# Row maxima of attention scores from 64 contraction rows, two heads as a pair of matmuls on the two halves of the rows

## What is computed

```python
k = jnp.concatenate([k_c, k_rb], axis=-1)      # 32 content + 32 position numbers per head
q = jnp.concatenate([q_c, q_rb], axis=-1)
scores = jnp.einsum('bhsd,bhtd->bhst', q, k) / math.sqrt(HEAD_DIM)
attn = jax.nn.softmax(scores, axis=-1)
ctx = jnp.einsum('bhst,bhtd->bhsd', attn, v_c)
```

## Time and profile before

| | |
|---|---|
| median of 3 runs | 1858.47 us (1858.25 to 1858.62) |
| the profiled execution | 1858.86 us |
| its span in the trace | 1857.0 us, so 1.9 us lie around it |
| mean granted TensorE clock | 0.946 of full speed |
| PE, DVE, ACT, POOL busy over the span | 92%, 56%, 45%, 39% |
| attention | from the start to about 1081 us |

### The profile page before, as it was taken

One profiled execution on the slowest core, in us unless ns is written; L12 is line 12 of the kernel. 1 busy time (PEld: TensorE's weight loads), 2 busy tenths in 40 slices (PEclk: granted clock), 3 DMA queues, 4 the chain that ended last, 5 costly groups with the idle time before them and its releaser, 6 DMA issues.

```text
span 1857.0 us, 21713 instructions
## 1 busy us (share of the span) xinstructions
PE 1703.8 (92%) x7194; PEld 1042.3 (56%) x7194; DVE 1030.8 (56%) x2133; ACT 828.4 (45%) x1465; POOL 726.6 (39%) x627
## 2 busy tenths in 40 slices
PE   5898989989989989989899788999999999988998
PEld 2444535435445445444444346888766666656886
DVE  2666577567676685684755635444511111116998
ACT  2345355355355454454454434443133333336554
POOL 0355465456455455563655642000122222214341
PEclk9798999989989999999989889999799999999999
DMA  5654455356355364462554332412473333448773
GB/s 157 174 155 123 121 143 181 84 152 181 86 165 152 93 187 123 136 190 77 150 162 150 100 114 79 164 46 97 132 264 131 126 127 132 127 141 299 240 240 123
DMA packets 123365, 270.51 MB, mean 146 GB/s; under 512 B 14996, under 2 KB 26644, under 8 KB 117108
## 3 DMA queue, kind: packets, MB, share of 16 engines
q1 hardware_dynamic: 96856, 205.93, 36.7%
q0 software_dynamic: 12912, 41.82, 7.1%
q10 hardware_dynamic: 13488, 21.37, 3.1%
HBM read 153.99 MB, written 92.01 MB: 132 GB/s over the span
## 4 chain that ended last, share of the span: by engine, by line
PE 66%; DVE 22%; DMA 4%; ACT 3%; issue 3%; POOL 1%; SPq 1%; DVEq 0%; ACTq 0%; POOLq 0%
PE bank L616 9%; PE bank L594 8%; PE bank L672 7%; PE bank L695 7%; DVE a L804 6%; PE bank L553 6%; PE bank L536 5%; PE bank L476 5%; DVE a L810 3%; PE bank L521 3%; PE bank L507 3%; PE bank L525 3%; PE bank L492 2%; PE bank L545 2%; DVE a L735 2%
## 5 line engine op out<-in xcount | busy, mean ns | idle before, releaser
L1449 POOL TENSOR_TENSOR a<-a 128x512 f32<-128x512 f32 x384 | 483.0, 1284 | 475.2 <-ACT a L1261 475.2
L1261 ACT ACTIVATE a<-bank 128x512 f32<-128x512 f32 x512 | 299.8, 595 | 258.2 <-PE bank L525 252.0
L804 DVE TENSOR_REDUCE a<-bank 128x1 f32<-128x512 f32 x512 | 325.2, 668 | 96.4 <-PE bank L507 95.9
L521 PE MATMUL bank<-a 128*128 128x512 f32 x512 | 281.6, 550 | 50.1 <-ACT a L1261 50.0
L507 PE MATMUL bank<-a 128*128 128x512 f32 x512 | 203.0, 434 | 28.5 <-DVE a L804 20.1
L525 PE MATMUL bank<-a 68*128 68x512 f32 x512 | 209.4, 409 | 0.3 <-ACT a L1251 0.2
L594 PE MATMUL bank<-c 128*128 128x512 f32 x768 | 186.8, 401 | 22.8 <-ACT c L1306 8.4
L521 PEld LDWEIGHTS bank<-a 128*128 128x128 f32 x512 | 100.1, 196 | 180.1 <-ACT a L1261 98.8
L1116 DVE TENSOR_TENSOR f<-f 128x256 f32<-128x256 f32 x79 | 33.6, 425 | 268.2 <-ACT f L1378 268.2
L594 PEld LDWEIGHTS bank<-c 128*128 128x128 f32 x768 | 146.2, 192 | 62.3 <-issue 13.2
L616 PE MATMUL bank<-c 128*128 128x512 f32 x768 | 176.8, 390 | 3.4 <-DVE c L854 1.7
(11 more groups left out here) (176 smaller groups left out, 2093.7 us busy)
## 6 DMA issues: line engine op xcount, KB each, us to landing
a<-kq_scratch SPq DMA_DIRECT2D x192, 256.0 KB, 5.6
kq_scratch<-a SPq DMA_DIRECT2D x32, 1024.0 KB, 4.1
a<-a SPq DMA_DIRECT2D x80, 256.0 KB, 5.0
yp_scratch<-f ACTq DMA_DIRECT2D x79, 256.0 KB, 2.0
a<-in_L_attn_x SPq DMA_DIRECT2D x15, 1024.0 KB, 8.5
x_scratch<-a SPq DMA_DIRECT2D x8, 1024.0 KB, 5.1
h_scratch<-a SPq DMA_DIRECT2D x8, 1024.0 KB, 4.3
hT_scratch<-a SPq DMA_DIRECT2D x8, 1024.0 KB, 6.5
```

The source lines that it names most:

```text
L521: e.matmul(SC[n % 2][:], K.Kc[:, z, j, i * P:(i + 1) * P], K.Qc[:, z, j, :], start=True, stop=False)
L804: e.tensor_reduce(K.mx[:, i, j:j + 1], K.MX[n % 3][:], AX.X, ALU.max).then_inc(Z.max, 1)
L1261: e.activation(K.pt[:, n % NP, :], K.SC[n % 2][:], ACT.Exp, scale=SCALE).then_inc(Z.exp, 1)
L1449: e.tensor_tensor(K.acc[:, j, :], a, K.pt[:, n % NP, :], ALU.add).then_inc(Z.acc, 1)
```

## The change

The first pass takes only high parts: 32 content rows and 32 position rows, 64 in all. The stacks are laid out by the parity of the head, so that an even head has these 64 rows in partitions 0 to 63 and an odd head has them in 64 to 127; the other half holds the two remaining products. A `top` now covers two heads: two matmuls of 64 rows, the first on the lower half and the second on the upper half of the rows, into two of the three banks. It waits once for the reduction that frees the second of the two banks, and DVE makes two reductions behind it. There are 8 pairs per unit in place of 16 tops. `scores` reads the same stacks as before, whose rows are only in another order. `send` issues 14 transfers in place of 8, with the same bytes.

```diff
+STACK = 14
 # attention_order, before the first unit and inside a unit
-    out += [("top", 0, j, i) for j in range(4) for i in range(4)] + [("rows", 0)] + norm_order("n", 1)
+    out += [("top", 0, j, i) for j in (0, 2) for i in range(4)] + [("rows", 0)] + norm_order("n", 1)
...
-        tops = [(j, i) for j in range(4) for i in range(4)] if u + 1 < NU else []
+        tops = [(j, i) for j in (0, 2) for i in range(4)] if u + 1 < NU else []
...
-            while nt < len(tops) and nt < (step + 1) * 5 // 4 + 2:
+            while nt < len(tops) and nt < (step + 1) * 5 // 8 + 1:
...
 # PE
     def top(u, j, i):
-        z, n = u % RS, 16 * u + 4 * j + i
-        if n >= 3:
-            w.wait_ge(Z.max, n - 2)
-        w.wait_ge(Z.stack[z], 8 * 16 * (u // RS + 1))
-        e.matmul(MX[n % 3][:], K.Qc[:, z, j, i * P:(i + 1) * P], K.Kc[:, z, j, :], start=True, stop=True).then_inc(Z.top, 1)
+        z, n = u % RS, 16 * u + 4 * j + 2 * i
+        if n:
+            w.wait_ge(Z.max, n - 1)
+        w.wait_ge(Z.stack[z], STACK * 16 * (u // RS + 1))
+        for c in range(2):
+            half = slice(64 * c, 64 * c + 64)
+            e.matmul(MX[(n + c) % 3][:], K.Qc[half, z, j + c, i * P:(i + 1) * P], K.Kc[half, z, j + c, :],
+                     start=True, stop=True).then_inc(Z.top, 1)
...
 # DVE
     def top(u, j, i):
-        n = 16 * u + 4 * j + i
-        w.wait_ge(Z.top, n + 1)
         if u:
             m = K.fill["rows", u - 1]
             w.wait_ge(Z.full[m % 2], m // 2 + 1)
-        e.tensor_reduce(K.mx[:, i, j:j + 1], K.MX[n % 3][:], AX.X, ALU.max).then_inc(Z.max, 1)
+        for c in range(2):
+            n = 16 * u + 4 * j + 2 * i + c
+            w.wait_ge(Z.top, n + 1)
+            e.tensor_reduce(K.mx[:, i, j + c:j + c + 1], K.MX[n % 3][:], AX.X, ALU.max).then_inc(Z.max, 1)
...
 # SP, send(u)
-        rep = lambda r: raw(K.krx[r:r + HD, y, :].unsqueeze(1).broadcast_to([HD, 4, S]))
+        rep = lambda r: raw(K.krx[r:r + HD, y, :].unsqueeze(1).broadcast_to([HD, 2, S]))
...
-        e.dma_start(raw(K.Kc[96:128, z, :, :]), rep(0)).then_inc(Z.stack[z], 16)
-        e.dma_start(raw(K.Qc[96:128, z, :, :]), rep(32)).then_inc(Z.stack[z], 16)
-        piece = lambda n: K.kq_d[z, :, n, :].rearrange("(j p) s -> p j s", j=4)
+        for t, r in ((K.Kc, 0), (K.Qc, 32)):
+            e.dma_start(raw(t[32:64, z, 0::2, :]), rep(r)).then_inc(Z.stack[z], 16)
+            e.dma_start(raw(t[64:96, z, 1::2, :]), rep(r)).then_inc(Z.stack[z], 16)
+        piece = lambda n, heads: K.kq_d[z, :, n, :].rearrange("(j p) s -> p j s", j=4)[:, heads, :]
         w.wait_ge(Z.kq[z], 16 * (u // RS + 1))
-        for t, k, n in ((K.Kc, 0, 0), (K.Kc, 1, 0), (K.Kc, 2, 1), (K.Qc, 0, 2), (K.Qc, 1, 3), (K.Qc, 2, 2)):
-            e.dma_start(raw(t[HD * k:HD * k + HD, z, :, :]), piece(n)).then_inc(Z.stack[z], 16)
+        even, odd, every = slice(0, 4, 2), slice(1, 4, 2), slice(0, 4)
+        for t, k, n, heads in ((K.Qc, 0, 2, every), (K.Kc, 0, 0, even), (K.Kc, 3, 0, odd), (K.Qc, 3, 2, every), (K.Kc, 0, 1, odd),
+                               (K.Kc, 1, 0, odd), (K.Qc, 1, 3, odd), (K.Kc, 2, 0, even), (K.Qc, 2, 3, even), (K.Kc, 3, 1, even)):
+            e.dma_start(raw(t[HD * k:HD * k + HD, z, heads, :]), piece(n, heads)).then_inc(Z.stack[z], 16)
```

More of the change, by code:

```diff
@@ L779, in proj @@
             u = NG * (b - 2) + 3
-            w.wait_ge(Z.stack[u % RS], 8 * 16 * (u // RS + 1))
+            w.wait_ge(Z.stack[u % RS], STACK * 16 * (u // RS + 1))
             w.wait_ge(Z.KR[z], 4 * 16 * (b // 2))
@@ L1572, in send @@
         if u >= RS:
-            w.wait_ge(Z.stack[z], 8 * 16 * (u // RS))
+            w.wait_ge(Z.stack[z], STACK * 16 * (u // RS))
         e.dma_start(K.kq_d[z], raw(K.kq[:])).then_inc(Z.kq[z], 16)
-        rep = lambda r: raw(K.krx[r:r + HD, y, :].unsqueeze(1).broadcast_to([HD, 4, S]))
+        rep = lambda r: raw(K.krx[r:r + HD, y, :].unsqueeze(1).broadcast_to([HD, 2, S]))
         w.wait_ge(Z.rope, 3 * (b + 1))
```

## The result

The changed kernel takes 1907.4 us in the median of five runs (1906.2 to 1932.1), the kernel before 1858.25, also of five: the ratio is 1.031 (1.024 to 1.037), 49 us slower. That lies outside the range of the prediction (1832 to 1890); the sign was right. The profiled execution is the longest of the five, 1932.1 us with a span of 1930.3; a second profile, of an execution of 1911.7 us, is among the experiments and is nearer to the median.

The account below looks back on a forecast made before the run. PE and DVE were taken to bound attention alternately. Pair edges 7 + unit start 5 + waits 1 + transfers 1.5 = +14.5 us on a median of 1858.5, so about 1873 us, range 1832 to 1890.

Parts of the forecast that it names:

- The bound: In attention PE and DVE alternate as bounds; 47% of the 512 tops lie on the path that sets the end.
- The pair on PE: Pair between two scores, side by side but paying edges: 1.07 us against 0.94, +0.13 each; before values -0.06 each.
- The terms of +7 and +5: +7 us: edges of the pairs on PE; +5 us: the pair at the start of 16 DVE-bound units.
- The crossing at the unit start: In DVE-bound units the chain crosses PE at half clock: 1.31 us with the pair against 0.98, +0.33, 16 units.
- The waits: PE's waits for reductions: never held later than before, only the first top's lead lost, mainly unit 0; +1 us, 0 to 3.
- The clock: PE's clock in attention should stay: stretches with waits at edges leave PE no more idle; no added time.
- The transfers: 14 transfers on SP instead of 8, delaying the first top in about 7 units: +1.5 us, bounds 0 and 18.
- Rival 2: On PE, edges paid, but the pair's second matmul runs after the first: 1907 us, chance 0.06.
- Rivals 1 and 3: On PE: rival 1, free edges, side by side, 1835 us, chance 0.26; rival 3, no special form, 1861 us, chance 0.12.
- rival 4: Small transfers are issued or land more slowly, more units wait: +18 on top of 14.5, 1891 us, chance 0.05.

Follow-up runs that it names:

- experiment 7: The changed kernel's stacks, but tops one at a time in their old places with old waits, each on 64 rows: 1934.3 us, ratio 1.041.
- late pairs: Pairs at the place of the old second top: 1907.4 us with half rows (the changed kernel), 1887.3 us with full 128-row matmuls.
- early ones: The changed kernel with each pair at the place of its first top instead of its second: 1892.0 us with half rows, 1886.5 with full 128-row matmuls.
- experiment 1: The changed kernel's order and waits, with the stacks, 8 transfers and 128-row matmuls of the kernel before: 1887.3 us, ratio 1.016.
- experiment 6: The kernel before, tops in old places, but the first of each two waits until two banks are free, the second for nothing: 1891.9 us, ratio 1.018.
- experiment 5: Pairs at the old second top's place with 128-row matmuls, as in experiment 1, but each top with its own old wait: 1879.5 us, ratio 1.012.
- experiment 2: The changed kernel's stacks and 14 transfers, with the 128-row tops, order and waits of the kernel before: 1856.3 us, ratio 1.000.

## Why the prediction was wrong

**The bound.** Right: PE and DVE alternate, and nothing after attention plays a part. That 47% of the tops are on the path took the path as fixed; experiment 7 has 61% for the edges.

**The pair on PE.** Right in every slot: side by side, 0.32 in, weights in the open, 0.43 and 0.34 out, 1.09 us against 1.07. The Trainium skill's rule (TensorEngine Tiling (Array Packing), "Key Properties"), that a change of tiling mode drains TensorE, agrees with the trace for rows too: 0.32 in and 0.43 out. The terms of +7 and +5 together made 12 us; the half rows cost 20 at late pairs (1907.4 less 1887.3) and 6 at early ones (1892.0 less 1886.5). Of the distance between late half rows and late full rows in the table, 25.9 us by the first profile and 9.1 by the second, 18.7 and 6.8 are in the fourth units, and in the second units, which PE bounds, it is 0.1. So outside the fourth units the half rows cost 7.2 or 2.3 us over these six batches, no more than the prediction had for the edges; most of what goes beyond it stands in the fourth units, with the clock. The crossing at the unit start is there, with 1.28 us for 1.31.

**The waits.** This is the step that failed. I wrote that a pair waits "exactly that for which the second top waited at the same place in the list", that "PE is thus never held later than before", and put +1 us on it; it is 31 us (experiment 1), the half clock behind the waits included. The semaphore's number is the same, but the reduction behind it isn't at the same place: on DVE the reduction of the first top has moved by up to a step, behind reciprocals and norm steps of several us. I took those fills for cover ("cover it"); they are what the reduction now waits behind. And the first top's lead, which I gave away as of use only in unit 0, is worth something in every batch: without it in the old places the kernel loses 35 us (experiment 6), with the late place and the old waits 23 (experiment 5). Even in unit 0 it was more than the +1: the sixteen reductions there, first start to last, take 11.6 us in the second profile instead of 9.0, 2.7 more, near the upper bound of 3.

**The clock.** The second failure, in one sentence of the sum: "stretches with waits at edges have PE no more idle than the column tiles do today". The granted clock over the span is 0.921 to 0.928 in the executions of the changed kernel, 0.946 before, where the prediction had it stay. In the fourth unit of a batch PE idles 1.65 and then 1.9 us, and where it does both, the clock is at half in the longest run of small matmuls. With work in the stalls of both kernels (mean clock 0.960 in both profiles) the distance is 1876.3 less 1847.4 = 29 us instead of 49, so by this estimate about 20 us are clock. It is rather a lower figure: the changed kernel also pays for 84 more matmuls in that comparison, and some of its fourth units are still long (38.9 us for unit 19). The remaining 29 are waits and edges, which the runs don't split further.

**The transfers.** +1.5 us was forecast, 0 was measured, the lower bound (experiment 2). Ten reads are issued in 5.03 us against six in 3.13, and, as the prediction had it, the issuing is not what ends it: counted from the issue of the 1 MB write, the last read is issued after 8.9 us instead of 6.9 and the last lands after 14.1 instead of 14.3 (medians of the 32 units).

```profile
138.05 0.34 SPq L1579 DMA_DIRECT2D kq_scratch<-a  x1
...
142.18 5.03 SPq L1592 DMA_DIRECT2D a<-kq_scratch  x10
```

**The rivals.** Rival 2 gave 1907 us, the time that was measured, by a mechanism that is not there: the two matmuls do run side by side. It is a coincidence and no credit to it. Rivals 1 and 3 fell with the slots, rival 4 with experiment 2. The rival that was missing is "the same wait number, but the reduction it counts has moved".

## What to carry to other kernels

When a step moves in a list that several engines follow, don't compare the numbers of the semaphores but the place of what they count on the engine that counts it, and list what now stands ahead of it there. Small independent matmuls that fit under each other still pay entry and exit at each change of form, so a pair that saves one stream of 0.21 us has to be put among its like, not alone between full ones. And what a short idle time of TensorE costs depends on what runs at half clock behind it: here a unit with one stall of 1.6 us took 35.0 us, no more than the kernel before, and with a second one of 1.8 us and half clock in the longest run of small matmuls behind it 41.6. Look at the granted clock by unit, before and after, and in more than one execution.

## What was not expected of the hardware

Two matmuls of 64 rows on different halves of the rows take 0.50 to 0.51 us together, where one alone has 0.49, but each change between them and the 128-row form costs, in all, 0.09 + 0.10 us at entry and 0.09 + 0.10 at exit. Matmuls added to a stall made the kernel before 10 us faster and the changed kernel 26 us, with clocks of 0.960 and 0.955 over the span against 0.946 and 0.921 to 0.928. And one program fell into executions of 1861 and of 1900 us; the two that were profiled differ in which of two stalls of a fourth unit the half clock follows.
